# Order of gathers and scatters, and w1 read in place, in a mixture-of-experts kernel

## What is computed

```
logits = gelu(x @ rw1) @ rw2                 # router, x layer-normalised
wgt, idx = top_k(softmax(logits), 2)
for e in range(8):
    Ye = gelu(x @ w1[e] + b1[e]) @ w2[e] + b2[e]      # w1[e] 256x1024, w2[e] 1024x256
    Ce = gelu(b1[e]) @ w2[e] + b2[e]                  # what a token gets that did not choose e
    for k in range(2):
        mask = idx[..., k] == e
        out += any(mask) * wgt[..., k] * where(mask, Ye, Ce)
```

## Time and profile before

| | |
|---|---|
| three runs | 244.8, 242.99, 244.16 us; median 244.16 |
| span of the profiled execution | 240.2 us, 5593 instructions |
| a run's time less that span | 2.8 to 4.6 us |
| busy: TensorE matmul, weight load | 174.1 us (72%), 141.8 us (59%) |
| busy: VectorE, ScalarE, GpSimd | 178.3 (74%), 96.2 (40%), 118.0 (49%) |
| chain that ended last, by engine | DVE 36%, PE 30%, DMA 14%, issue 10% |
| the same by line, its largest | gathers' DMA into `probT` 8% |
| mean granted TensorE clock | 0.876 of 2.4 GHz |

### The profile page before, as it was taken

How to read it: one execution, slowest core, us unless ns; L and a number is a source line. 1 busy time by engine, 2 the same in 40 slices (tenths; PEclk the granted TensorE clock), 3 DMA queues, 4 the chain that set the end, 5 groups by cost and what they waited for, 6 DMA issues and landing times.

```text
span 240.2 us, 5593 instructions
## 1 busy us (share of the span) xinstructions
PE 174.1 (72%) x1708; PEld 141.8 (59%) x1709; DVE 178.3 (74%) x352; ACT 96.2 (40%) x230; POOL 118.0 (49%) x144
## 2 busy tenths in 40 slices
PE   7876638818500176729997989989797979799691
PEld 2455426317400133629887979889797979687370
DVE  1399998999999899596956776767675767656264
ACT  1369527656585700603333342423333334233000
POOL 0033365991789209992337282746455464632100
PEclk9997988976855557779999999999999999999955
DMA  7893564785887504101001111110102020100096
GB/s 190 280 381 118 175 213 145 249 282 193 271 302 256 189 3 130 45 1 46 20 21 46 44 44 32 32 55 15 57 22 66 20 66 22 46 15 27 31 289 233
DMA packets 20625, 28.05 MB, mean 117 GB/s; under 512 B 2341, under 2 KB 17407, under 8 KB 20610
## 3 DMA queue, kind: packets, MB, share of 16 engines
q1 hardware_dynamic: 16768, 21.94, 27.6%
q0 software_dynamic: 1872, 4.73, 6.3%
q10 hardware_dynamic: 1970, 1.19, 1.8%
HBM read 23.64 MB, written 4.60 MB: 118 GB/s over the span
## 4 chain that ended last, share of the span: by engine, by line
DVE 36%; PE 30%; DMA 14%; issue 10%; POOL 3%; ACT 2%; POOLq 2%; SPq 1%; DVEq 0%; ACTq 0%
DMA probT<-x_table,gcol 8%; PE bank L1065 4%; DVE lnx L562 4%; PE bank L1066 4%; PE bank L1067 4%; PE bank L1075 4%; PE bank L1077 4%; PE bank L1076 4%; DVE w_lo L539 4%; DMA xs<-in_x 4%; DVE cf L765 2%; POOL gcol L326 2%; DMA stage<-y_table 2%; DVE prob L588 2%; ACT w_hi L399 2%
## 5 line engine op out<-in xcount | busy, mean ns | idle before, releaser
L512 ACT ACTIVATE lnx<-bank,b1T 128x128 f32<-128x128 f32 x152 | 43.3, 367 | 78.6 <-PE bank L1067 72.2
L316 POOL TENSOR_TENSOR w_lo<-stage,w_hi 128x1024 bf16<-128x1024 f32 x23 | 50.3, 2212 | 35.2 <-ACT w_hi L399 35.1
L1065 PE MATMUL bank<-cfT,stage 128*128 128x128 f16 x272 | 52.6, 219 | 0.0
L1066 PE MATMUL bank<-cfT,stage 128*128 128x128 bf16 x272 | 52.6, 219 | 0.0
L1067 PE MATMUL bank<-cfT,stage 128*128 128x128 f16 x272 | 52.6, 219 | 0.0
L1075 PE MATMUL bank<-w_hi,cf 128*128 (+1 forms) x152 | 41.8, 275 | 5.6 <-DVE lnT L767 5.5
L1077 PE MATMUL bank<-w_hi,lnT 128*128 (+1 forms) x152 | 41.7, 275 | 0.0
L1076 PE MATMUL bank<-w_lo,cf 128*128 (+1 forms) x152 | 41.7, 274 | 0.0
L399 ACT ACTIVATE w_hi<-stage 128x1024 f16<-128x1024 f32 x32 | 32.4, 1051 | 20.1 <-DMA stage<-in_L_ffn_w 17.5
L322 POOL TENSOR_TENSOR held<-cst 128x1 f32<-128x1 f32 x39 | 12.1, 310 | 47.1 <-DVE qT L774 44.8
L1065 PEld LDWEIGHTS bank<-cfT,stage 128*128 128x128 f16 x272 | 26.6, 98 | 1.5
(11 more groups left out here) (168 smaller groups left out, 321.6 us busy)
## 6 DMA issues: line engine op xcount, KB each, us to landing
stage<-in_L_ffn_w SPq DMA_DIRECT2D x32, 512.0 KB, 4.1
stage<-y_table SPq DMA_DIRECT2D x8, 256.0 KB, 4.2
xs<-in_x SPq DMA_DIRECT2D x1, 1024.0 KB, 8.4
out<-stage SPq DMA_DIRECT2D x4, 256.0 KB, 3.5
cf<-in_ctx SPq DMA_DIRECT2D x1, 512.0 KB, 4.7
x_table<-cfT ACTq DMA_DIRECT2D x2, 256.0 KB, 2.6
x_table<-probT ACTq DMA_DIRECT2D x2, 256.0 KB, 4.2
probT<-x_table,gcol POOLq DMA_INDIRECT x20, 2.8
```

Source lines behind the costliest of these rows:

```text
L316: nc.gpsimd.tensor_tensor(out=w_lo[:, q, :], in0=stage[:, q % RING, :], in1=w_hi[:, q, :], op=ALU.subtract).then_inc(lo_pool, 1)
L512: last = nc.scalar.activation(hidden[u][:, cc * P:cc * P + P], bank[(0 if u == 0 else 6) + half][:, c * P:c * P + P], ACT.Gelu, bias=b1T[: ...
L1065: mm(o, wh, xh[:, d, :], start=(d == 0), stop=False)
L1066: mm(o, wh, xl[:, d, :], start=False, stop=False)
```

## The change

GpSimd's order becomes gather (j+1, 0), scatter (j-1, 0), gather (j+1, 1), scatter (j-1, 1), with the edges to match: both scatters of pair 0 stand ahead of the loop, pair 1 of GpSimd falls away, and the tail scatters (jl-1, 0), (jl-1, 1), (jl, 0) and, where there is one, (jl, 1). VectorE's `fetch_w1`, its semaphore and its waits for the weights go. TensorE loads three experts' numbers per pair in place of two, and `up` reads `w_hi` and `w_lo` at a register's address.

```diff
-            def pair(j, first=False, last=False):
-                if first:
-                    for u in range(2):
-                        wait(tr_x, u + 1)
-                        wait(gathered[u], 16)
-                        gather(2, u)
-                elif not second(j) and not last:
-                    for u in range(2):
-                        wait(tr_x, 2 * j + u + 1)
-                        wait(gathered[u], 16 * j)
-                        gather(j + 1, u)
-                if first:
-                    wait(index_ready, 2)
-                else:
-                    if not isinstance(j, int) or j > 1:
-                        wait(scattered[1], 16 * (j - 1))
-                    scatter(j - 1, 1)
-                    wait(scattered[0], 16 * j)
-                scatter(j, 0)
-
-            pair(0, first=True)
-            pair(1)
+            def refill(j, u):
+                wait(tr_x, 2 * j + u + 1)
+                wait(gathered[u], 16 * j)
+                gather(j + 1, u)
+
+            def put(j, u):
+                if not isinstance(j, int) or j:
+                    wait(scattered[u], 16 * j)
+                scatter(j, u)
+
+            def pair(j):
+                refill(j, 0)
+                put(j - 1, 0)
+                refill(j, 1)
+                put(j - 1, 1)
+
+            for u in range(2):
+                wait(tr_x, u + 1)
+                wait(gathered[u], 16)
+                gather(2, u)
+            wait(index_ready, 2)
+            for u in range(2):
+                put(0, u)
...
-            pair(jl, last=True)
+            for u in range(2):
+                put(jl - 1, u)
+            put(jl, 0)
             with pool.If(2 * jl + 1 < used):
-                wait(scattered[1], 16 * jl)
-                scatter(jl, 1)
+                put(jl, 1)
...
-            def fetch_w1(i, u):
-                e = dve.value_load(eb[0:1, bass.ds(i, 1)], min_val=0, max_val=N_EXP - 1)
-                if not isinstance(i, int) or i > 3:
-                    dve.wait_ge(h_done, 2 * i - 2)
-                for h in range(2):
-                    nc.vector.tensor_copy(w1f[:, u, h, :].bitcast(I32).unsqueeze(1),
-                                          w1_words[h][:, bass.ds(e, 1), 0:QW]).then_inc(w1_fetched, 1)
...
-                fetch_w1(2 * j + 1, 1)
...
-                fetch_w1(2 * j + 2, 0)
...
-            experts = [pe.alloc_register(f"expert_{n}") for n in ("before", "even")]
+            experts = [pe.alloc_register(f"expert_{n}") for n in ("before", "even", "odd")]
...
-                    if e is None:
-                        pe.wait_ge(w1_fetched, 2 * i - 2)
...
-                    if e is None:
-                        wh, wl = w1f_hi[u][:, d, cs], w1f_lo[u][:, d, cs]
-                    else:
-                        wh, wl = w1_hi[:, bass.ds(e, 1), d, cs], w1_lo[:, bass.ds(e, 1), d, cs]
+                    wh, wl = w1_hi[:, bass.ds(e, 1), d, cs], w1_lo[:, bass.ds(e, 1), d, cs]
...
-                    up(2 * j, 0, None, c)
+                    up(2 * j, 0, eb_, c)
...
-                    up(i + 1, 1, None, c)
+                    up(i + 1, 1, ec, c)
```

More of the change, by code:

```diff
@@ L67, in flamingo_moe_kernel @@
         stage = sb("stage", [P, RING, QW], F32)
[L69 to L74, removed]
         y_in = stage[:, :, :].rearrange("p a (b n) -> p (a b) n", n=D)
@@ L211, in flamingo_moe_kernel @@
         dlg_ready, elg_ready = sem("dlg_ready"), sem("elg_ready")
-        w1_fetched = sem("w1_fetched")
         gcol_ready, ycol_ready = sem("gcol_ready"), sem("ycol_ready")
@@ L815, in _ @@
             hidden_split(0, 0, 1)
-            wait_weights(dve, QUARTERS - 5)
-            fetch_w1(2, 0)
             hidden_split(0, 1, 0)
@@ L840, in pair @@
                 hidden_split(j, 0, 1)
-                fetch_w1(2 * j + 2, 0)
                 hidden_split(j, 1, 0)
                 y_copy(j, 0)
-            wait_weights(dve, QUARTERS - 3)
             pair(1)
-            wait_weights(dve, QUARTERS - 1)
             dve.wait_ge(used_ready, 1)
@@ L854, in _ @@
             hidden_split(jl - 1, 1, 1)
-            fetch_w1(2 * jl + 1, 1)
             hidden_split(jl, 0, 0)
@@ L1095, in first_half @@
             def first_half(j):
-                ea, eb_ = [pe.snap(r, min_val=0, max_val=N_EXP - 1) for r in experts]
+                ea, eb_, ec = [pe.snap(r, min_val=0, max_val=N_EXP - 1) for r in experts]
                 tokens_tr(j, 1)
                 for c in range(HC):
-                    up(2 * j, 0, None, c)
+                    up(2 * j, 0, eb_, c)
                     down(2 * j - 1, 1, ea, c)
-                return eb_
+                return eb_, ec
             def pair(j):
                 i = 2 * j
-                eb_ = first_half(j)
+                eb_, ec = first_half(j)
                 load_experts(j + 1)
@@ L1119, in _ @@
                     pair(j)
-            eb_ = first_half(jl)
+            eb_, ec = first_half(jl)
             def residual_to(q):
@@ L1127, in _ @@
                 for c in range(HC):
-                    up(2 * jl + 1, 1, None, c)
+                    up(2 * jl + 1, 1, ec, c)
                     down(2 * jl, 0, eb_, c)
-                el = expert_of(2 * jl + 1)
                 residual_to(0)
                 for c in range(HC):
-                    down(2 * jl + 1, 1, el, c)
+                    down(2 * jl + 1, 1, ec, c)
             with pe.Else():
```

## The result

The changed kernel takes **264.17 us**, the median of 4 runs (262.97 to 265.52), against 243.57 for the kernel before in the same comparison (4 runs, 242.26 to 244.8). The ratio is **1.085**, 95% interval 1.079 to 1.092: slower by 20.6 us. The forecast was 264.7, with a range of 253 to 277.

A forecast was written before the change was run, and what follows sets the result against it. TensorE, nearly the bound, gives way to its instruction queue: pair 1 +3.0, seven pairs +16.8, last half pair +0.7, sum 20.5 over 240.2, plus 4.0 around the span, 264.7 us; own range 258 to 272, wider range 253 to 277.

The forecast's parts named there:

- The bound changes from TensorE to its queue: Expert loop: register operations make a unit 0.73 us in TensorE's queue, where TensorE itself needs 0.66.
- The groups add up: Each unit's two up groups and one down group carry register operations; their queue times add, 3 x 0.243 = 0.73 us.
- The estimate by the Trainium skill: Queue price if firmware handles each matmul at about 62 ns: 264 ns a group, total about 273 us.
- the marking that the same section reports: Matmuls bypass the sequencer's firmware, so a group costs only its two register operations; leads to the faster rival, 233 us.
- The seams come into the open: Branch and load work between half pairs, formerly hidden by TensorE's backlog, shows: 1.05 and 1.75 us, pair 14.9 us.
- The order is worth at most 1.58 us per pair: GpSimd's new order removes TensorE's wait for the gather in the loop: at most 11.1 us over seven pairs.
- Pair 1: First pair of the loop: pair 2 begins at 128.0 instead of 124.97, +3.0 us.
- the seven pairs: Pairs 2 to 8 of the loop: 105.3 us against 88.5, +16.8, including 1.0 for leaving the loop.
- Rival 3: Much slower: TensorE's clock halves after the loop's seams, 20 us more at most, 270 to 285 us; chance 0.07.
- The tail: Last half pair to the end: up groups take 5.5 us against 4.81, +0.7; nothing changes from there on.
- TensorE's matmul busy time in a pair: In the table by stage, TensorE's matmul busy time in a loop pair stays unchanged at 11.2 us.
- What lies around the span: Median of three runs lies 4.0 us above the profiled span of 240.2; added to the forecast span of 260.7.

The follow-up runs named there:

- experiment 3: Changed kernel with the down products reading w2 of expert 0 at a fixed address, four register operations per unit: 235.15 us, ratio 0.963 to the kernel before.
- experiment 4: Changed kernel, but VectorE copies w1's low part and only the high part is read in place, four register operations per unit: 240.62 us, ratio 0.985.
- experiment 6: Changed kernel, but the second of a unit's two up groups reads a copied low part, five register operations per unit: 252.25 us, ratio 1.034.
- experiment 9: Changed kernel with one up matmul per unit reading a slice nothing else uses, seven register operations per unit: 281.12 us, ratio 1.150.
- experiment 7: Changed kernel with a register move in place of the third expert load per pair: 260.91 us, ratio 1.072 to the kernel before.
- experiment 1: Kernel before with only GpSimd's new order of gathers and scatters, w1 still copied: 233.01 us, ratio 0.953.
- 10: Changed kernel with the up products reading w1 of expert 0 at fixed addresses, no copies on VectorE: 235.38 us, ratio 0.963.
- experiment 11: Changed kernel without the branch and code for an odd last block in TensorE's stream: 263.66 us, ratio 1.0785.
- 8: Changed kernel with one up matmul per unit reading the next unit's w1 slice; the builder shared the address, still six operations: 265.02 us, ratio 1.088.
- 2: Changed kernel with GpSimd's old order, so only the reading of w1 in place is new: 264.40 us, ratio 1.083.

## Why the prediction was right

**The bound changes from TensorE to its queue.** Right. Before, the down group alone had operations; experiments 3, 4, 6 and 9 change their number, and the time follows it. In 3, 4 and 6 fewer matmuls have a register's address at the same time; experiment 9 changes the number of operations and, but for which data are read, nothing else.

**The groups add up.** This was the step with which the forecast stood or fell, since no row showed three together. By the pair's own balance, with the seams as forecast, (14.67 - 1.05 - 1.75 - 0.4) / 48 = 0.239 us per group; the queue itself starts groups 0.24 apart at 165 us, and experiment 9 gives 0.123 for a single operation. The 0.24 read off holds. The estimate by the Trainium skill, "TensorE: Matmul & The Clock Gate", section "Wait — 56ns, not 53.3ns?", with 62 ns per matmul, was 0.264 and 15.9 us a pair; the measured 14.67 is below it. By the marking that the same section reports, as going straight to the engine, the time would have been 233, and that too does not describe these products: with their operations and instructions in the queue they are paced at 0.24 us for three, where three with fixed addresses go at 0.17 (144.68 to 144.85 in the kernel before).

**The seams come into the open.** Right in place and nearly in size: pair 14.67 against 14.9 forecast, the third load 0.46 to 0.50 in the queue, and 0.42 net of a move (experiment 7), against 0.5.

**The order is worth at most 1.58 us per pair.** Right: 88.53 - 77.94 = 10.6 in seven pairs, 1.51 each, alone (experiment 1), and nothing beside the read in place (experiment 2), as the forecast's sum has it. **The copies are worth 0.** Right (experiments 1 and 10).

**Pair 1** came out at +3.04 against +3.0, **the seven pairs** at +15.95 against +16.8. **Rival 3** did not come: the clock stayed at 1.00 with a gap of 1.2 and one of 0.4 us in each pair.

Of the forecast's terms and signs, these were off:

- **The tail**, "From there on (...) nothing changes", +0.7. It measured +2.65. The last up groups, 240.11 - 234.35 = 5.76 us against 4.81, gave +0.95. From the last up group to the copy of y it is 245.70 - 240.11 = 5.59 us, where 222.86 - 218.31 = 4.55 stood before, +1.04: nearly all of this is the branch over the odd block's code, 1.168 us where it was 0.355 (0.9 goes with it in experiment 11). I had taken the branch as unchanged, because its condition and its place are. The remaining 0.66 lies behind the last copy of y, 18.0 us against 17.4; over all kernels here this stretch is 17.4 to 18.8 without any order, so it need not be the change's.
- **The seven pairs**, +16.8, measured +15.95. The pair was put 0.2 too long, and the leaving of the loop with the slower first two pairs takes 1.8 us where 1.0 was added.
- **TensorE's matmul busy time in a pair**, forecast as unchanged at 11.2. It is 13.07 with the same matmuls. A matmul is shown with a modelled duration of 0.22 us; where its successor starts 0.06 later the two overlap, and where the queue lets the successor come later the duration covers the gap, so that only the two seams, 1.17 and 0.42 us, show as idle. A busier TensorE in such a profile is not more work. The rest of what would show it came as listed: 288 operations, units 0.72 to 0.74 apart, idle put to issue, gathers 8 us early, no copies.
- **What lies around the span**, 4.0. A run's time less its own span is 1.8 us in all four of the changed kernel and 1.8 to 2.6 in those of the kernel before beside it and the experiments. The rest of the 4.0 was that the profiled execution was faster than the median of its kernel. For a forecast of the median the step was sound, with four runs of the kernel before 3.4 instead of 4.0.

So the total was closer than its parts. In medians the change was forecast at +20.5 and measured at +20.6: the seven pairs 0.85 too long, the tail 1.3 to 1.95 too short, and the rest within what one execution differs from another. That the two cancel so nearly is luck; the mechanism and its size in the loop are not.

## What to carry to other kernels

Count what the engine's queue has to do in a unit of work, each register operation here at about 0.12 us, and set it against the engine's own time for the unit: well below it the operations, loads and branches cost nothing, above it all of them are paid, and a copy to a fixed address by an engine with idle time is the cheaper read. Two changes made together are to be priced one at a time, since the one that creates a new bound can swallow the other's gain: here the order alone gives 233.0 us against 244.1, and both give 264.2. Before taking more code into a branch that is skipped, look at what the skip costs.

## What the runs showed that was not expected

- **A skipped branch takes from 0.35 to 3.9 us of the queue**, with no change of its condition or its data: 0.355 us before, 0.352 and 0.353 in experiments 1 and 3, 0.373 in 9, 0.471 in 8, 0.777 in 10, 1.108 in 2, 1.168 in the changed kernel, 1.228 in 7, 1.956 in 6, 3.874 in 4. What TensorE loses is what its backlog does not cover: from the last up group to the copy of y it is 4.55 to 4.62 us in the kernel before and experiments 1 and 10, 4.77 and 4.82 in 8 and 9, 5.5 to 5.7 with the branches of 1.1 to 1.2, 6.20 in 6 and 9.05 in 4. The length is not in order of the code skipped: experiment 9 has more of it than the changed kernel and pays a third. Nor does a short branch mean that nothing is lost: in experiment 3 TensorE stops for 1.28 us a little behind it, between two matmuls with fixed addresses, and its copy of y comes 5.72 us after the last up group. Fetching of instructions that the queue has not yet at hand would fit; it was not tested and stays open.
- **After the gap of 2.83 us in experiment 4** TensorE ran at half the clock for 3.4 us (216.9 to 220.3), while the gap of 1.66 us at the same place in experiment 6, and gaps of 1.2 us in each pair, left it at 1.00.
- **The price is a threshold, not a slope**: the third and fourth operation together cost 0 to 0.14 us per pair, the fifth 1.6.
